# Weighted edge sums in a four-layer graph network: messages weighted and split first, then summed by two float32r products

## What is computed

```python
def _L1_gnn_ref(h, weight, edge_weight, src, dst):
    hp = h @ weight
    msgs = hp[src] * edge_weight[:, None]
    agg = jax.ops.segment_sum(msgs, dst, num_segments=h.shape[0])
    return jax.nn.relu(agg)
...
x = _layernorm(x + _L0_gnn_ref(...))
x = _layernorm(x + _L1_gnn_ref(x, L1_gnn_weight, edge_weight, src, dst))
x = _layernorm(x + _L2_gnn_ref(...))
x = _layernorm(x + _L3_gnn_ref(...))
```

## Time and profile before

| what | value |
|---|---|
| median of 3 runs | 2253.58 us (2251.02 to 2253.9) |
| the profiled execution's own time | 2249.59 us |
| its span, first to last instruction | 2247.9 us |
| mean granted TensorE clock | 0.991 |

### The profile page before, as it was taken

The page is one execution under the profiler, slowest core; times in us unless marked ns, Lnnn a source line. Parts: engine busy times, 40 slices in busy tenths (PEclk is TensorE's granted clock), DMA queues, the critical chain, the costliest instruction groups (busy, mean ns, idle before and its releaser), DMA issues.

```text
span 2247.9 us, 36380 instructions
## 1 busy us (share of the span) xinstructions
PE 2199.6 (98%) x12269; PEld 1888.6 (84%) x12269; DVE 1487.8 (66%) x4615; ACT 1024.2 (46%) x2028; POOL 937.4 (42%) x931
## 2 busy tenths in 40 slices
PE   8999999979999999999999999999999999999997
PEld 6878878858899888888999999988888777888785
DVE  8777878744767856666326666267776777678675
ACT  5982112222366632222224656344434666676454
POOL 2017637745222234376552223013444554753542
PEclk9999999989999999999999999999999999999998
DMA  6434665443476748787225667356667777776442
GB/s 215 148 133 136 161 194 193 150 137 106 138 249 216 275 151 278 254 285 252 84 92 175 221 225 258 108 187 227 218 219 236 252 251 246 246 256 227 164 124 69
DMA packets 192495, 435.82 MB, mean 194 GB/s; under 512 B 45751, under 2 KB 74622, under 8 KB 191774
## 3 DMA queue, kind: packets, MB, share of 16 engines
q1 hardware_dynamic: 127034, 249.08, 32.2%
q0 software_dynamic: 65296, 184.67, 26.3%
HBM read 242.68 MB, written 190.96 MB: 193 GB/s over the span
## 4 chain that ended last, share of the span: by engine, by line
PE 72%; DVE 2%; DMA 1%; ACT 1%; issue 1%; POOL 0%; POOLq 0%; SPq 0%; ACTq 0%; DVEq 0%
PE g_h_ps L2625 7%; PE g_h_ps L2642 7%; PE g_h_ps L2627 7%; PE g_h_ps L2626 7%; PE g_h_ps L2643 6%; PE g_h_ps L2644 6%; PE g_h_ps L2667 6%; PE g_h_ps L2669 5%; PE g_h_ps L2668 5%; PE g_t_ps L80 4%; PE g_h_ps L1783 2%; PE g_h_ps L1785 2%; PE g_h_ps L1784 2%; PE g_sum_ps L1023 1%; PE g_sum_ps L1022 1%
## 5 line engine op out<-in xcount | busy, mean ns | idle before, releaser
L2764 ACT ACTIVATE g_act_t<-g_t_ps,g_b_col 128x256 f32<-128x256 f32 (+1 forms) x488 | 202.0, 466 | 371.9 <-PE g_t_ps L80 371.7
L2642 PE MATMUL g_h_ps<-g_x_hi,held_w_hi 128*128 128x256 f32 x1216 | 352.5, 290 | 0.0
L2643 PE MATMUL g_h_ps<-g_x_lo,held_w_hi 128*128 128x256 f32 x1216 | 344.2, 283 | 0.0
L2644 PE MATMUL g_h_ps<-g_x_hi,held_w_lo 128*128 128x256 f32 x1216 | 344.1, 283 | 0.0
L632 DVE CUSTOM_DVE_ANT_0 g_prod<-g_h_sb,g_a_rows 128x256 f32<-128x256 f32 x632 | 224.3, 419 | 79.7 <-ACT g_h_sb L513 71.9
L2667 PE MATMUL g_h_ps<-fc_w_hi,g_x_hi 128*128 128x512 f32 x632 | 268.8, 425 | 2.1 <-DVE g_x_lo L2943 2.1
L2625 PE MATMUL g_h_ps<-held_w_hi,g_x_hi 128*128 128x512 f32 x656 | 264.0, 402 | 0.0
L2627 PE MATMUL g_h_ps<-held_w_hi,g_x_lo 128*128 128x512 f32 x656 | 257.2, 392 | 0.0
L2626 PE MATMUL g_h_ps<-held_w_lo,g_x_hi 128*128 128x512 f32 x656 | 257.1, 392 | 0.0
L2669 PE MATMUL g_h_ps<-fc_w_hi,g_x_lo 128*128 128x512 f32 x632 | 247.5, 392 | 0.0
L2668 PE MATMUL g_h_ps<-fc_w_lo,g_x_hi 128*128 128x512 f32 x632 | 247.0, 391 | 0.0
(11 more groups left out here) (401 smaller groups left out, 4834.2 us busy)
## 6 DMA issues: line engine op xcount, KB each, us to landing
h<-g_h_sb SPq DMA_DIRECT2D x120, 512.0 KB, 3.6
h<-g_rows_own SPq DMA_DIRECT2D x40, 512.0 KB, 4.8
g_x_in<-in_dram SPq DMA_DIRECT2D x39, 512.0 KB, 3.9
h_cols<-g_h_sb SPq DMA_DIRECT2D x38, 512.0 KB, 4.9
xb_rows<-in_dram SPq DMA_DIRECT2D x19, 1024.0 KB, 6.1
xb<-xb_rows SPq DMA_DIRECT2D x19, 1024.0 KB, 4.4
g_x_in<-h_cols SPq DMA_DIRECT2D x38, 512.0 KB, 7.6
g_x_in<-h SPq DMA_DIRECT2D x21, 512.0 KB, 6.4
```

What stands on the lines that cost most here:

```text
L2642: pe.matmul(out, wh, xh, start=(k == 0), stop=False)
L2643: pe.matmul(out, wh, xl, start=False, stop=False)
L2644: last = pe.matmul(out, wl, xh, start=False, stop=(k == KC - 1))
```

## The change

The edge weight moves from the mask to the message. ScalarE multiplies each source row by its edge weight and rounds the result to float32r (`message`, into `msg_hi`); VectorE forms the same product again and subtracts the rounded one (`rest`, into `msg_lo`); TensorE multiplies the 0/1 mask, which is exact in float32r, with both. `weigh` and its buffers are gone. `msg_hi` and `msg_lo` exist once each, in place of a bias table that is no longer read. `sum_edges` waits for `rest`, no longer for the gather, and `message` takes that wait over, one step earlier. The semaphore `carried` now counts carries and messages.

```diff
     def sum_edges(self, pe, t):
         h = self.hold
         pe.wait_ge(self.weighed, t + 1)
-        pe.wait_ge(self.x_in[t % 4], 32 * (t // 4 + 1))
         if t:
 
-            pe.wait_ge(self.carried, t)
             pe.wait_ge(self.sums_out, t)
-        pe.matmul(h.sum_ps, h.weighted[t % 2][:, :], h.x_src[t % self.ROWS], start=True, stop=True).then_inc(self.summed, 1)
+        mask = h.mask[:, t * P:(t + 1) * P]
+        pe.matmul(h.sum_ps, mask, h.msg_hi[:, :], start=True, stop=False)
+        pe.matmul(h.sum_ps, mask, h.msg_lo[:, :], start=False, stop=True).then_inc(self.summed, 1)
...
+    def message(self, act, t):
+
+        h = self.hold
+        act.wait_ge(self.x_in[t % 4], 32 * (t // 4 + 1))
+        if t:
+
+            act.wait_ge(self.carried, 2 * t)
+            act.wait_ge(self.summed, t)
+        act.activation(h.msg_hi[:, :], h.x_src[t % self.ROWS], ACT.Copy,
+                       scale=h.tabs[:, t, D_EW:D_EW + 1]).then_inc(self.carried, 1)
...
-    def weigh(self, dve, t):
-        h = self.hold
-        if t >= 2:
-
-            dve.wait_ge(self.summed, t - 1)
-        dve.tensor_scalar(h.weighted[t % 2][:, :], h.mask[:, t * P:(t + 1) * P].bitcast(F32), h.tabs[:, t, D_EW:D_EW + 1],
-                          None, ALU.mult).then_inc(self.weighed, 1)
+    def rest(self, dve, t):
+
+        h = self.hold
+        dve.wait_ge(self.carried, 2 * t + 1)
+        dve.scalar_tensor_tensor(h.msg_lo[:, :], h.x_src[t % self.ROWS], h.tabs[:, t, D_EW:D_EW + 1],
+                                 h.msg_hi[:, :].bitcast(F32), ALU.mult, ALU.subtract).then_inc(self.weighed, 1)
...
+                    if g == CONV - 2:
+                        conv.message(act, 0)
                     n = conv_step(g)
                     if n is not None:
                         if 0 <= n + 1 < ET:
                             conv.round_sums(act, n + 1)
                         if 0 <= n + 2 < ET:
                             conv.copy_sums(act, n + 2)
+                        if 1 <= n + 3 < ET:
+                            conv.message(act, n + 3)
...
-                    if g == CONV - KC:
-                        conv.weigh(dve, 0)
-                        conv.weigh(dve, 1)
+                    if g == CONV - 2:
+                        conv.rest(dve, 0)
                     n = conv_step(g)
                     if n is not None:
-                        if 2 <= n + 3 < ET:
-                            conv.weigh(dve, n + 3)
                         if 0 <= n < ET:
                             conv.add_own(dve, n)
                         if 0 <= n + 1 < ET:
                             conv.split_sums(dve, n + 1)
                         if 0 <= n < ET:
                             conv.factors(dve, n)
+                        if 1 <= n + 3 < ET:
+                            conv.rest(dve, n + 3)
```

More of the change, by code:

```diff
@@ L1711, in __init__ @@
         self.rest_done, self.rests_before = conv.weighed, ET
-        self.carry_rest_done, self.carries_before = conv.carried, ET - 1
+        self.carry_rest_done, self.carries_before = conv.carried, 2 * ET - 1
         self.b_in = sem("mlp_b_in")
@@ L2031, in node_layers @@
         a_rows = sb("a_rows", [P, 2, HC])
+        b_rows_at = sb.end
         b_rows = sb("b_rows", [P, 2, D])
@@ L2133, in node_layers @@
         low = Space(nc, "conv", rest_at)
-        c.weighted = [low(f"weighted{s}", [P, P]) for s in range(2)]
         c.stats = [low(f"stats{s}", [P, 2, 6]) for s in range(2)]
@@ L2138, in node_layers @@
         c.log_d, c.rstd, c.shift = ([low(f"{n}{s}", [P, 3]) for s in range(2)] for n in ("log_d", "rstd", "shift"))
+        early = Space(nc, "conv", b_rows_at)
+        c.msg_hi, c.msg_lo = early("msg_hi", [P, D], F32R), early("msg_lo", [P, D], F32R)
+        assert early.end <= tile_at
         c.w_raw, c.mask, c.tabs, c.ident, c.index = fc_raw, e.mask, tabs, ident, e.index
```

## The result

| kernel | median (us) | runs |
|---|---|---|
| before | 2252.10 (2249.72 to 2253.90) | 8 |
| after | 2259.68 (2258.10 to 2264.29) | 8 |

The changed kernel is slower by 7.6 us: the ratio is 1.0035, with a 95% interval of 1.0024 to 1.0046. The profiled execution after the change took 2260.64 us, with a span of 2258.2 us and a mean granted TensorE clock of 0.988.

What follows compares the result with a forecast made beforehand. The prediction took a ScalarE-VectorE ring, as tight as TensorE, to bound the edge layer: 8.3 - 0.8 - 1.3 = +6.2 us, taken as +6 on 2253.6, rounded to 2259.5 us; range 2249 to 2264 us.

Steps and rivals of the forecast that it cites:

- the ring: Edge layer: ScalarE and VectorE wait for each other from one `round_sums` to the next, 7.51 us a round from tile 6.
- 8.3 less 2.1: Ring's end in the edge layer: 8.3 us pushed by `rest`, less 0.8 and 1.3 us, giving +6.2 us.
- The ring is a second bound, as tight as TensorE: Edge layer: 7.51 us a round on ScalarE and VectorE against TensorE's step of 7.44 us; no faster in thirteen of twenty rounds.
- TensorE saves 0.40 us a step: Sum on TensorE: two float32r products take 0.46 us where the float32 product took 0.86; 8.0 us in 20 steps.
- `rest` pushes the ring in thirteen rounds by 0.61 us and in rounds 3, 4, 6 and 7 by 0.1: VectorE between `factors` and `shifts`, rounds 1 to 17: four rounds have an idle gap, thirteen have none; 8.3 us in all.
- 0.8 us and 1.3 us come off at the start and where waits for TensorE close: `round_sums(1)` comes two sums earlier, 0.8 us; later waits of ScalarE and VectorE for TensorE can close, 1.3 us.
- `weigh` removed gives nothing: VectorE before `add_own`: 0.28 us a step removed, counted as nothing because VectorE mostly waits for `round_sums` afterwards.
- the rival of the hardly pushed ring: Removed `weigh` counts, or small waits in the groups' work absorb `rest`: +2.2 us, 2255.8 us; chance 0.33.
- `message` is hidden: ScalarE before `root`: 0.62 us fits into a 1.28 us average wait for VectorE, costing nothing; rival unhidden, 2264.5 us, chance 0.07.
- TensorE's saving turns into waits, and nothing is given back later: TensorE waits out its 8.0 us and 6 more; the third layer's first gather waits for the last stored rows.
- The Trainium skill's rule: Rival: TensorE, busy 159.5 of 160 us, is the bound and its 8.0 us arrive, 2245.6 us; chance 0.12.

Runs made afterwards that it cites:

- the products alone: Kernel before, only the float32 sum product replaced by two float32r products of mask and weight rows (sums are other numbers); 2248.62 us, ratio 0.9995.
- the two opened kernels: Kernels before and after, each with `root`, `shifts` and `normalize` of a tile one step later, stores and gathers too; 2248.15 and 2241.63 us.
- `rest` alone: Kernel before plus one VectorE operation of the kind, size and place of `rest`, into an unread spare buffer, steps 0 to 16; 2255.80 us, ratio 1.0024.
- the run with it alone: Kernel before plus one ScalarE operation of the kind, size and place of `message`, into an unread spare buffer, tiles 1 to 19; 2250.11 us, ratio 0.9997.
- `rest` behind `shifts`: Changed kernel with `rest` moved, from tile 3 on, from behind `factors` to behind `shifts` on VectorE; 2252.57 us, ratio 1.0009.
- `rest` first: Changed kernel with `rest` for the tile summed in this step put at the step's start on VectorE, before `add_own`; 2256.56 us, ratio 1.0026.
- the ring opened: Changed kernel with `root`, `shifts` and `normalize` of a tile one step later, the layer's stores and gathers too; 2241.63 us, ratio 0.9965.

## Why the prediction was right, point by point

The forecast was 2259.5 us, and 2259.68 us was measured. The mechanism is the one it named. That the times agree to 0.2 us is luck: the forecast added 6 us to a base of 2253.6 us, and what came was 7.6 us on a base of 2252.1. In the ring the forecast was 8.3 less 2.1, and 7.8 less 0.8 came: both terms were too large, and their errors partly cancel.

- *The ring is a second bound, as tight as TensorE.* Shown: the products alone gain nothing that can be told from none, and only opening the ring lets the sum's saving through. TensorE enters the ring at a second place, which the prediction did not name: `add_own` waits for the product, 7.8 us in 7 waits in the stretch before the change. It set nothing, because VectorE waited for `round_sums` behind each of the seven.
- *TensorE saves 0.40 us a step.* It is 0.37, by the rounds of the two opened kernels. The two products do not start 0.23 us apart, as I had said, but 0.32: the first one holds TensorE longer, the second 0.23 us. The sum also starts 0.09 us sooner behind the turn (0.35 us after it, not 0.44), which I had not counted.
- *`rest` pushes the ring in thirteen rounds by 0.61 us and in rounds 3, 4, 6 and 7 by 0.1.* `rest` takes 0.67 us. Eleven of the thirteen rounds (2, 5, 8 to 15 and 17) grew, by 7.1 us together, 0.64 on average; round 16 grew by 0.27 and round 1, in which TensorE still led, by 0.02. Of the four covered rounds 4, 6 and 7 grew by 0.07, 0.06 and 0.30. That is 7.8 us where the forecast had 8.3: rounds 1 and 16 took away 0.9 us, and the longer `rest` added only 0.4. Less the two rounds of the next point the 19 rounds grew by 7.03 us.
- *0.8 us and 1.3 us come off at the start and where waits for TensorE close.* Rounds 0 and 3 became 0.37 and 0.38 us shorter, 0.75 us in all and not 2.1. The first sum came 0.47 us later against the slots around it than before (its `message` waited 1.1 us for the gather, and TensorE 0.3 us for `rest`), which took its own saving back. Here I had counted on cover.
- *`weigh` removed gives nothing.* `rest` alone, with `weigh` kept, makes the ring longer by 7.4 us, the whole change by 7.0, of which the shorter sum explains 0.3. With 0.1 us for `message` that leaves some 0.2 us for `weigh` in all rounds together, if the parts add up, and the eleven rounds grow as much with `weigh` as without it. So the rival of the hardly pushed ring, which gave it 0.28 a round, is refuted.
- *`message` is hidden.* Shown by the run with it alone.
- *TensorE's saving turns into waits, and nothing is given back later.* TensorE waits 9.0 us for `split_sums`, where the forecast had 14 (its own 8.0 and 6 more). Some 3.4 us of the rest went into the lower clock: behind two of these waits nine products each start 0.42 us apart on average and not 0.23 (1795.67 to 1799.42 and 1836.53 to 1840.28). The third layer's first gather follows `round_sums(19)` at the same distance.

The Trainium skill's rule in Perfetto Trace Analysis, section "Identifying the Most-Contended Engine", to optimize the engine of the highest occupancy first, would have brought the prediction's whole 8 us. This case does not agree: +7.6 us, where TensorE had been busy for 159.5 of 160 us. It agrees in the opened kernels, where TensorE waits for nothing and its shorter step arrives.

Open: by the ratios the kernels with both `message` and `rest` end 0.9 to 2.4 us above what their rings say (the changed kernel: +7.0 in the ring, +7.9 in the time; `rest` behind `shifts`: +0.3 and +2.0; `rest` first: +3.6 and +5.9; the ring opened: -10.3 and -7.9). Part of that, some 0.7 us, lies outside the span: a run's time less its span is 2.0 to 2.5 us in all 39 runs of these four kernels and 1.7 to 1.8 us in all runs of the others; what it is no trace shows. In three of the four profiles TensorE also waits 1.2 to 1.5 us for the third layer's first gathered rows, where it waits for 0 to 0.5 us in the kernels without both; why these rows land later was not tried. What is left is within what the intervals leave open: the kernel with `rest` alone ends 2.0 us below its ring.

## What to carry to other kernels

Full occupancy of one engine does not make it the only bound: follow one round of the other engines from an operation to its next occurrence, and compare that time with the full engine's step. If both are equal, a saving on the full engine is worth next to nothing (here 0.3 us of some 7 in the rounds), and an operation costs its whole length where it stands between the waits that the ring is made of and next to nothing where it stands in a gap; so first take the ring apart (here by consuming each tile's statistics one step later), then shorten the full engine's step. When an operation is moved into a gap, ask who reads its result and when.

## What was unexpected of the hardware

The granted TensorE clock fell for a moment after some of the new waits. The windows view of the changed kernel, in steps of 5 us (PEclk is the third number from the end):

```profile
1785.00:1790.00 5.00, 5.00 (x25) 4.14 (x25) 4.83 (x13) 1.49 (x4) 3.68 (x4) 1.00 0.72 203
1790.00:1795.00 5.00, 2.96 (x13) 2.09 (x12) 2.02 (x7) 4.23 (x7) 1.66 (x2) 1.00 0.58 184
1795.00:1800.00 5.00, 4.33 (x12) 3.42 (x13) 4.79 (x15) 3.34 (x8) 3.27 (x4) 0.66 0.89 279
...
1830.00:1835.00 5.00, 4.45 (x22) 3.39 (x20) 2.55 (x11) 2.81 (x5) 2.01 (x3) 1.00 0.96 360
1835.00:1840.00 5.00, 3.47 (x9) 2.73 (x10) 4.08 (x13) 3.21 (x9) 3.78 (x5) 0.68 0.81 250
```

After TensorE had waited for 2.70 and 2.08 us the clock averaged 0.66 and 0.68 in the windows that follow or hold the wait: a part of each at the lower level of 1.2 GHz, where the products start 0.43 us apart and not 0.23, and where the stretch before the change stood at 1.00. It did no harm here, because TensorE was the one that waited: the two rounds of the fall (6 and 11) take 6.86 and 7.69 us, and the same 6.86 and 7.69 us in the kernel with `rest` alone, where the clock stayed at 1.00. Where TensorE comes to lead, the fall costs on top of the wait: in the run with `rest` first, after a wait of 2.51 us, TensorE's step was 1.6 us longer for it, and ScalarE waited 2.08 us for the turn.
